# A linear-attention block with norms: the query scores of a tile moved up in TensorE's order, right behind its key scores

## The reference, cut to what matters

```python
h = _layernorm(x, axis=-1) * (1 + ca) + sa
Q = heads(Wq) / math.sqrt(dk)
K = heads(Wk) / math.sqrt(dk)
V = heads(Wv)
...
xw = jnp.einsum('bhtd,hmd->bhtm', x, proj)          # for Q and for K: the "scores"
xw = xw - jnp.max(xw, axis=-1, keepdims=True)
x_norm_sq = jnp.sum(x * x, axis=-1, keepdims=True)
return jnp.exp(xw) * jnp.exp(-0.5 * x_norm_sq) + EPS
...
KV = jnp.einsum('bhtm,bhtd->bhmd', phiK, V)
```

## Time and profile before

| what | value |
|---|---|
| time, median of 3 runs | 1911.62 us (1908.49 to 1914.94) |
| profiled execution, its own time | 1913.27 us |
| its span | 1911.5 us |
| PE busy | 1727.4 us (90%) |
| DVE busy | 1408.2 us (74%) |
| ACT busy | 1105.7 us (58%) |
| POOL busy | 1139.8 us (60%) |

### The profile page before, as it was taken

The page is one execution under the profiler, slowest core; times in us unless marked ns, Lnnn a source line. Parts: engine busy times, 40 slices in busy tenths (PEclk is TensorE's granted clock), DMA queues, the critical chain, the costliest instruction groups (busy, mean ns, idle before and its releaser), DMA issues.

```text
span 1911.5 us, 31887 instructions
## 1 busy us (share of the span) xinstructions
PE 1727.4 (90%) x11562; PEld 989.8 (52%) x11562; DVE 1408.2 (74%) x2643; ACT 1105.7 (58%) x2066; POOL 1139.8 (60%) x1062
## 2 busy tenths in 40 slices
PE   5599979999899888999979987999997999799997
PEld 4477544444377644444447754444435775444443
DVE  4598768777578796777748877777756887677774
ACT  0388434656568643566648854356665884346664
POOL 0487236766858424766768722576676861377665
PEclk7799999999999998999989999899998999999999
DMA  4000143001110026002020004500111001430101
GB/s 129 0 2 2 37 146 91 18 10 42 56 34 2 1 93 166 23 10 51 1 88 2 2 1 141 132 9 17 42 34 56 2 2 46 153 75 17 33 19 45
DMA packets 55717, 87.45 MB, mean 46 GB/s; under 512 B 13316, under 2 KB 32004, under 8 KB 52868
## 3 DMA queue, kind: packets, MB, share of 16 engines
q1 hardware_dynamic: 55560, 85.40, 15.6%
HBM read 47.20 MB, written 35.70 MB: 43 GB/s over the span
## 4 chain that ended last, share of the span: by engine, by line
PE 69%; DVE 13%; ACT 10%; POOL 4%; issue 3%; SPq 1%; POOLq 0%; DMA 0%; ACTq 0%; DVEq 0%
PE PS L1311 12%; PE PS L1457 11%; PE PS L1445 9%; PE PS L1209 6%; DVE MXP L979 6%; PE PS L1470 6%; PE PS L1389 3%; PE PS L1234 3%; PE PS L1217 3%; PE PS L1244 3%; ACT HT L591 2%; ACT HTR L594 2%; PE PS L1360 2%; PE PS L1379 2%; PE PS L1224 1%
## 5 line engine op out<-in xcount | busy, mean ns | idle before, releaser
L560 POOL TENSOR_TENSOR TS<-PR 128x1024 f32<-128x1024 f32 (+1 forms) x256 | 573.3, 2239 | 298.6 <-ACT PR L777 281.1
L979 DVE TENSOR_REDUCE MXP<-PS 128x1 f32<-128x512 f32 x960 | 598.0, 681 | 177.7 <-PE PS L1311 174.3
L777 ACT ACTIVATE PR<-PS 128x512 f32<-128x512 f32 x960 | 504.6, 602 | 360.9 <-PE PS L1445 357.6
L1311 PE MATMUL PS<-KOP,QOP 96*128 96x512 f32 x960 | 421.1, 451 | 43.5 <-DVE MXP L979 41.9
L1445 PE MATMUL PS<-QOP,KOP 97*128 97x512 f32 x960 | 377.9, 407 | 12.6 <-ACT PR L777 12.6
L1311 PEld LDWEIGHTS PS<-KOP,QOP 96*128 96x128 f32 x960 | 185.3, 194 | 305.3 <-DVE MXP L979 208.6
L1457 PE MATMUL PS<-PR,V 128*32 128x512 f32 x1920 | 273.4, 606 | 0.0
L1445 PEld LDWEIGHTS PS<-QOP,KOP 97*128 97x128 f32 x960 | 180.6, 191 | 78.1 <-ACT PR L777 50.2
L1470 PE MATMUL PS<-TS,ones 128*32 128x512 f32 x960 | 133.2, 593 | 5.4 <-POOL TS L560 5.4
L1209 PE MATMUL PS<-W1T,HTR 128*128 128x512 f32 x384 | 116.3, 442 | 21.8 <-POOL HTR L449 21.8
L1244 PE MATMUL PS<-PB,QKT 64*128 64x256 f32 x1536 | 124.9, 295 | 0.7 <-DVE QKT L910 0.4
(11 more groups left out here) (153 smaller groups left out, 2658.3 us busy)
## 6 DMA issues: line engine op xcount, KB each, us to landing
KOP<-k_scr SPq DMA_DIRECT2D x84, 256.0 KB, 6.8
k_scr<-QKS SPq DMA_DIRECT2D x64, 256.0 KB, 3.1
QOP<-q_scr SPq DMA_DIRECT2D x180, 64.0 KB, 2.0
q_scr<-QKS SPq DMA_DIRECT2D x40, 256.0 KB, 2.8
X<-in_L_attn_x_dram SPq DMA_DIRECT2D x16, 512.0 KB, 4.7
out_dram<-X SPq DMA_DIRECT2D x16, 512.0 KB, 3.1
QOP<-MXT SPq DMA_DIRECT2D x224, 0.5 KB
KOP<-QKS SPq DMA_DIRECT2D x36, 64.0 KB, 2.0
```

What stands on the lines that cost most here:

```text
L560: g.tensor_tensor(sums(k)[:, 0:len(stage)], pair[:, :, 0], pair[:, :, 1], ALU.add).then_inc(S["psum_t"], 1)
L777: a.activation(PR[:, k % 2, w, q], bank(score_bank(p, n, w, q)), ACT.Exp).then_inc(S["ex"], 1)
L979: v.tensor_reduce(MXP[:, u % 2, i, kc:kc + 1], bank(max_bank(p)), AX.X, ALU.max).then_inc(S["am_rd"], 1)
L1311: mm(bank(max_bank(p)), QOP[0:96, u % QS6, i * P:(i + 1) * P], KOP[0:96, h % KS6, kc * CH:(kc + 1) * CH], start=True, stop=True).then_inc( ...
```

## The change

On PE, in `tile` of the feature stage, the call that does the query scores of the tile is moved from behind the projection of the next tile to right behind the key scores. Every instruction stays; no semaphore, buffer or other engine's program is changed.

```diff
                     feature_scores(n, at, 0, 1, "xwk", "xk_sb")
+                    feature_scores(n, at, 2, 0, "xwq", "xq_sb")
                     if at >= 2:
                         query_features(b, t - 2, 1, at - 2)
                     if at < NT - 1:
                         project(b, t + 1, at + 1)
-                    feature_scores(n, at, 2, 0, "xwq", "xq_sb")
                     if at < NT - 1:
                         project_values(b, t + 1, at + 1)
                         qk_transposes(b, t + 1, at + 1)
```

## The result

| what | before | after |
|---|---|---|
| time, median | 1910.05 us (1906.01 to 1914.94, 4 runs) | 1934.38 us (1933.07 to 1935.10, 4 runs) |
| ratio | | 1.0116, 95% interval 1.0098 to 1.0133 |
| profiled execution, its span | 1911.5 us | 1933.1 us |

The account below looks back on a forecast made before the run. The feature stage was taken to run at a 7.30 us loop through PE, ACT and POOL, growing 0.83 a tile. A stage loses 11.3 us, four 45; 1912 + 45 = 1957, taken as 1956, range 1938 to 1967.

Parts of the forecast that it names:

- What bounds the stage: Feature stage: a loop of 1.65 from key scores to projection plus 5.65 to the next key scores, 7.30 us a tile.
- the 5.65 behind the projection: From projection to next key scores: 5.65 us of latency in a row on ACT, POOL and PE, kept after the change.
- From a projection: 1.70 to ACT's copy; 3.02 from that copy to DVE's low part: First two terms of the new loop over `XSQ`; the 3.02 was taken as ACT's own work in a row.
- The sum 8.13: New period from projection to projection: 1.70 + 3.02 + 0.67 + 1.21 + 0.13 + 0.90 + 0.50, so 0.83 us a tile more.
- Tile 0 ... nothing.: First tile of a stage: its projection starts long after its key scores, so the query scores fit ahead; no change.
- Tile 1: Second tile of a stage: projection at 85.65 where it was 85.10, a loss of 0.55 us.
- The wait for `XSQ`: Moved query scores wait for `xq_sb` from DVE's `XSQ`, so they can start 1.08 us after the key scores.
- latency alone: Rival: `XSQ` doesn't hold the query scores; 0.65 us a tile, 1947, or 1940 with pieces spared at joins; chance 0.18.
- PE as the bound, and the spared drain: Rival: PE's work bounds; joined score blocks spare idles of 0.37 and 0.17 a tile, 1882, or 1902 with only 0.17; chance 0.05.
- The signs: Middle tile: wrong if period stays below 7.6, projection comes sooner than 2.2 after key scores, or loss shows in other stages.
- The clock in the steady stage: Rival: PE idles about 1 us in 8, clock falls to 1.2 GHz, at least 1.27 a tile, 2022 or above; chance 0.03.

Follow-up runs that it names:

- Half of the block: Against the kernel before, the first 6 of 12 query scores stand early with the wait for `xq_sb`, the other 6 in the old place: 1916.67 us, ratio 1.0014.
- the block behind the turns: Against the changed kernel, the query scores stand one place later, behind the turns and still ahead of the projection: 1952.12 us, ratio 1.0202 (1.0173 to 1.023).
- the wait alone: Against the kernel before, only PE's wait for `xq_sb` is put right behind the key scores; the scores stay: 1913.45 us, ratio 1.0003.
- the changed kernel with the squares moved: Against the changed kernel, ACT's square of `QK` is moved behind its copies to `V` and `QKT`: 1917.91 us, ratio 1.0037 to the kernel before.
- another kernel: Against the kernel before, query scores early in tiles 1 to 15, in the old place in tile 0: 1934.98 us, ratio 1.0118.

## Why the prediction was right in its direction and wrong in its size

- **What bounds the stage.** Right in the main: a loop with 1.65 from key scores to projection, and the rest behind it. Half of the block and the block behind the turns moved the period with the projection's distance from the key scores; the wait alone moved neither. But the 5.65 behind the projection was called latency "on ACT, POOL and PE", in which "PE must wait for ACT and POOL anyway", and PE never waited there. The rows of before between the values and the next key scores show no idle of PE:

```profile
103.21 0.60 PE L1224 MATMUL PS<-ident,QK 128*128 128x128 f32 x4
...
103.64 0.60 PE L1234 MATMUL PS<-ident,XSQ 128*128 128x128 f32 x4
...
104.08 0.38 PE L1199 MATMUL PS<-ident,XH 128*128 128x128 f32 x2
...
104.85 0.62 PE L1258 MATMUL PS<-PK,ones 128*32 128x128 f32 x16
```

So 5.65 was PE's own work in a row as well. With all or half of the query scores out of that stretch it took 5.48 to 5.53, and the 0.16 a tile that came back in the changed kernel was not in the forecast.

- **The step that failed: "From a projection: 1.70 to ACT's copy; 3.02 from that copy to DVE's low part".** The sum 8.13 was made of distances in the old order, taken for fixed latencies. It came out as 1.67 + 2.85 + 0.66 + 1.22 + 0.05 + 0.91 + 0.41 = 7.77. The 3.02 was not "ACT's own work in a row": ACT's copy to `QKT` stood 0.37 behind its copy to `V` then (103.47 to 103.84), right after PE's turns of `QK`, which ended at 103.21 + 0.60 = 103.81; it stands 0.26 behind it now, and those turns are long done (102.43 + 0.64 = 103.07). Copy to exponential was 0.53, with DVE's `XSK` ending 0.03 ahead of the exponential, and is 0.49. DVE to PE was taken as 0.13 from the second tile's key scores, and is 0.05. The turns were taken at 0.50, but the projection behind them had waited for POOL's `HTR`, which ended at 99.69; they take 0.41. Four of the seven readings were too long by 0.03 to 0.17, and none was too short by more than 0.01: 0.36 a tile, 0.36 x 13 x 4 = 18.7 us.
- **"Tile 0 ... nothing."** Wrong by a sign of its own: 1.34, 1.33, 1.41 and 1.39 us less in the four stages (9.48, 9.02, 9.32, 9.31 to 8.14, 7.69, 7.91, 7.92), 5.5 us. The row of 2.93 at the lower level was used, for the fear that the clock might fall; that the same row was a price already paid in each stage, and that the moved block would fill the idle ahead of it, was missed.
- **Tile 1.** 0.55 forecast, 0.15 measured (7.22 to 7.37): 1.6 us. With the others 18.7 + 5.5 + 1.6 = 25.8; from the forecast's 45.4 that leaves 19.6, and the stages show 19.8.
- **The wait for `XSQ`.** Right in place: it is in the trace, and taking it out gave 0.25. The rival "latency alone" had 0.65 a tile left without it; 0.22 were left. The loss came out smaller than even that rival's (1940 to 1947), but not by its condition, since the wait was there.
- **PE as the bound, and the spared drain.** The time did not fall, so this rival is out as it was told, but it was not empty: PE's own work was as long as the loop, as said above, and the join of the blocks spares something where nothing stops them. A block of 12 scores between work of other kinds takes 0.90 until the next starts (101.34 to 102.24), and two in a row take 1.62 (112.88 to 114.50 in the changed kernel with the squares moved), which is 0.18 less than twice 0.90. This agrees with the rule on changes of tiling mode that the prediction cites from the Trainium skill (TensorEngine Tiling (Array Packing), Tiling Modes, Key Properties); no run separates a drain from other costs of such a change. In the changed kernel the stop for `XSQ` takes the gain back: 0.96 and 0.91.
- **The signs.** Neither sign of being wrong came: the period is not below 7.6 (7.77), and the projection not sooner than 2.2 after the key scores (2.28). DVE waits for ACT before the low part, as foretold. ACT's idle before the copy of the projection did not grow to 1.6: it is 0.79, and another 0.53 stands ahead of its copy to `PHIQ` (100.38), for which the turns now come late.
- **The clock in the steady stage** stayed at 1.00.

## What to carry to other kernels

When a busy engine and a loop have the same length, moving work on that engine to a place where others wait for it costs time even with the engine's work unchanged: here 0.47 us a tile for a block of 0.90, and 0.86 one place later. Sum such a loop from the shortest distance that each pair shows anywhere in the trace, and keep the one in the tile at hand as the other bound: a distance in a tight schedule often holds a second wait. And treat the first pass of a loop by itself: work moved into an idle ahead of the first matmuls there can pay through the clock, and of the versions here the one with the lowest time moved the block in that pass alone (ratio 0.9954 to the kernel before).

## What was not expected of the hardware

In the kernel before (two traces) and in that with the wait alone, TensorE ran the first projection at the 1.2 GHz level in 12 of 12 stages, with an idle of only 1.1 to 1.5 us ahead of it, and in none of 24 with 12 more matmuls there. With the same idle (1.54 and 1.35 us) it stayed at the 2.4 GHz level in two of four stages of another kernel. Six projection matmuls take 2.93 us at the one level and 1.66 at the other.
